# First products of two experts for half the batches computed ahead, and a new written order on all engines, in a one-core Mamba and Soft-MoE layer

## The reference, cut to what matters

```python
h = _layernorm(x) * (1 + ca) + sa
x = x + ga * mamba(h)              # in-projection, conv of 4 taps, silu, decay, out-projection
h = _layernorm(x) * (1 + cb) + sb
xn = rmsnorm(h); sn = rmsnorm(slot_embeds)
logits = einsum('bnd,esd->bnes', xn, sn)
dispatch = softmax(logits, axis=1); combine = softmax(logits over e and s)
slots = einsum('bnd,bnes->besd', xn, dispatch)
h = gelu(einsum('besd,edh->besh', slots, w1) + b1)      # the "first products", 128 -> 512
eo = einsum('besh,ehd->besd', h, w2) + b2
x = x + gb * einsum('bmd,bnm->bnd', eo, combine)
```

## Time and profile before

| | |
|---|---|
| median of 3 runs | 234.22 us (234.08 to 236.19) |
| profiled execution, its own time | 231.47 us |
| its span (first to last instruction) | 229.5 us |
| PE busy | 208.5 us, 91% of the span |
| DVE busy | 138.8 us, 60% |
| ACT busy | 120.3 us, 52% |
| POOL busy | 60.8 us, 26% |
| second pass, about | 84 to 155 us of the span |
| stage two, about | 155 to 212 us |

### The profile page before, as it was taken

How to read it: one execution, slowest core, us unless ns; L and a number is a source line. 1 busy time by engine, 2 the same in 40 slices (tenths; PEclk the granted TensorE clock), 3 DMA queues, 4 the chain that set the end, 5 groups by cost and what they waited for, 6 DMA issues and landing times.

```text
span 229.5 us, 4239 instructions
## 1 busy us (share of the span) xinstructions
PE 208.5 (91%) x1575; PEld 150.0 (65%) x1575; DVE 138.8 (60%) x364; ACT 120.3 (52%) x264; POOL 60.8 (26%) x147
## 2 busy tenths in 40 slices
PE   3898988996789899998996799989999999999995
PEld 2544565665458695565664478776774947759995
DVE  3795869799899966878889784730040220402663
ACT  2869898531557875699530666647417053270000
POOL 6443886015632401886015610000000000000000
PEclk9999997999999999999999999999999999999999
DMA  6404000300320000000600000005222142200122
GB/s 186 118 4 140 1 0 5 94 3 0 124 106 3 0 0 0 4 0 2 188 0 1 0 3 0 0 3 171 60 57 80 49 121 64 69 26 0 49 69 69
DMA packets 15344, 10.72 MB, mean 47 GB/s; under 512 B 1773, under 2 KB 13654, under 8 KB 15326
## 3 DMA queue, kind: packets, MB, share of 16 engines
q1 hardware_dynamic: 15100, 10.31, 14.9%
q10 hardware_dynamic: 226, 0.16, 0.3%
HBM read 9.34 MB, written 1.07 MB: 45 GB/s over the span
## 4 chain that ended last, share of the span: by engine, by line
PE 71%; DVE 11%; ACT 10%; DMA 3%; issue 2%; POOL 1%; ACTq 1%; DVEq 0%
PE bank L577 30%; PE bank L922 12%; PE bank L904 11%; PE bank L761 4%; PE bank L814 3%; PE bank L750 2%; DVE xcT L1310 2%; ACT zsT L1067 2%; PE bank L829 2%; DMA vec_nat<-ffn_slot_norm_gamma_dram 1%; ACT xhT L1073 1%; PE bank L835 1%; PE bank L860 1%; PE bank L883 1%; ACT L1067 1%
## 5 line engine op out<-in xcount | busy, mean ns | idle before, releaser
L1445 DVE TENSOR_TENSOR eo<-bank,seg_e 128x512 f32<-128x512 f32 x8 | 5.5, 692 | 47.9 <-PE bank L922 47.9
L922 PEld LDWEIGHTS bank<-w_sb,zsT 128*64 128x64 f32 x256 | 27.8, 137 | 3.0 <-issue 3.0
L922 PE MATMUL bank<-w_sb,zsT 128*64 128x128 f32 x256 | 28.8, 273 | 0.0
L922 PE MATMUL bank<-w_sb,xcT 128*64 128x128 f32 x256 | 28.8, 273 | 0.0
L922 PEld LDWEIGHTS bank<-w_sb,xcT 128*64 128x64 f32 x256 | 27.8, 137 | 0.0
L904 PE MATMUL bank<-slotsT,w_sb 128*128 128x512 f32 (+1 forms) x64 | 26.1, 558 | 0.2 <-ACT zsT L1141 0.2
L1141 ACT ACTIVATE zsT<-bank,vecT 128x512 f32<-128x512 f32 x16 | 10.7, 687 | 24.9 <-PE bank L904 24.9
L577 PE MATMUL bank<-xnT,winT 128*128 128x512 f32 x48 | 23.0, 607 | 0.7 <-ACT BT L1054 0.7
L490 POOL TENSOR_TENSOR root<-root,neg_half 128x2 f32<-128x2 f32 (+1 forms) x24 | 20.3, 847 | 2.0
L904 PEld LDWEIGHTS bank<-slotsT,w_sb 128*128 128x128 f32 x64 | 11.4, 190 | 12.6 <-issue 12.1
L1310 DVE SCALAR_TENSOR_TENSOR xcT<-bank,convw,xcT 128x510 f32<-128x510 f32 (+2 forms) x24 | 17.3, 736 | 3.6 <-ACT xcT L1051 3.3
(11 more groups left out here) (165 smaller groups left out, 423.7 us busy)
## 6 DMA issues: line engine op xcount, KB each, us to landing
w_sb<-in_L_ffn_w_dram SPq DMA_DIRECT2D x16, 256.0 KB, 2.9
mods_bc<-mod_dram SPq DMA_DIRECT2D x4, 320.0 KB, 3.6
xin<-in_L_attn_x_dram SPq DMA_DIRECT2D x4, 256.0 KB, 3.1
out_dram<-x1tok SPq DMA_DIRECT2D x16, 64.0 KB, 1.5
mods_bc<-mod_dram SPq DMA_DIRECT2D x4, 192.0 KB, 3.2
seg_e<-mod_dram SPq DMA_DIRECT2D x1, 512.0 KB, 3.4
eo<-in_L_attn_in_proj_w_dram SPq DMA_DIRECT2D x1, 384.0 KB, 4.2
eo<-in_L_wmod_dram SPq DMA_DIRECT2D x1, 256.0 KB, 5.1
```

The lines of the kernel that those rows point to most:

```text
L922: q = nc.tensor.matmul(o[j * S:(j + 1) * S, tile_cols(b)], act_h[j][k // 2][:, k % 2, at:at + S], w2_sb[j][:, k, :], start=k == 0 and b == ...
```

## The change: what it does

1. For experts 2 and 3 (round 1 of stage two) the first products of batches 0 to 3 are made in the second pass, on PE, by `ahead_hidden(0)` and `ahead_hidden(1)`: 4 products of 256 columns each, into banks 2 and 3, and banks 6 and 7. ACT's `copy_ahead` copies the four banks to SBUF, into x's and xnT's buffers, which are free by then. In stage two `hidden(1)` makes only the other 256 columns, and ACT's `gelus` makes two activations of 256 columns where it made one of 512.
2. The two weight tiles for this are loaded by two more DMAs into xntok's buffers, ahead of the first loads of w1 in SP's list.
3. `parts` keeps its remainder in the PSUM bank instead of SBUF.
4. The turns of all five tables are new, with some waits that the new orders need (`wait_before` in three steps; `logits(0)` of the second pass waits for `copy_ahead`).

```diff
+        AHEAD, AHEAD_B = 2, B // 2
+        w1_ahead = [t[:, :, :].rearrange("p t d -> p (t d)") for t in xntok]
+        pre = [t[:, :, :].rearrange("p t d -> p (t d)") for t in xin], [t[:, :] for t in xnT]
...
+            for j in range(2):
+                wait(sp, xnT_ps, j, PASSES - 1)
+                sp.dma_start(w1_ahead[j], w1[AHEAD + j:AHEAD + j + 1, :, :].rearrange("o d h -> d (o h)")
+                             ).then_inc(w1_ahead_in[1][j], 16)
...
                         wait(pe, seg_done, j, it)
+                        if it == PASSES - 1:
+                            wait(pe, pre_done, j, 0)
...
+            def ahead_hidden(j):
+                def visit():
+
+                    wait(pe, seg_done, j, PASSES - 1)
+
+                    for i in range(2):
+                        wait(pe, slotsT_done, i, 0)
+                    wait(pe, w1_ahead_in, j, 0)
+                    for k in range(HC):
+                        q = mm(bank[4 * j + 2 + k // 2][:, tile_cols(k % 2, AHEAD_B * S)], w1_ahead[j][:, tile_cols(k)],
+                               slotsT[:, AHEAD + j, 0:AHEAD_B, :].rearrange("p b s -> p (b s)"))
+                        if k % 2:
+                            q.then_inc(pre_ps[1][j], 1)
+                return visit
...
-                    b0 = EARLY if it == 0 and j == 0 else 0
+                    e = it * 2 + j
+                    b0 = EARLY if e == 0 else AHEAD_B if e in (AHEAD, AHEAD + 1) else 0
...
+            def copy_ahead(j):
+                def visit():
+                    for n in range(HC // 2):
+                        wait(act, pre_ps, j, 0, n + 1)
+                        if j == 0:
+                            wait(act, basis_done, n, PASSES - 1)
+                        A(pre[j][n], bank[4 * j + 2 + n][:, :], ACT.Copy).then_inc(pre_done[1][j], 1)
+                return visit
...
-                        wait(act, hid_ps, j, it, k + 1)
-
+                        o, at = act_h[j][k // 2][:, k % 2, :], 0
                         if it:
                             act.wait_ge(eo_ps, 2 * it)
-                        A(act_h[j][k // 2][:, k % 2, :], bank[k][:, :], ACT.Gelu,
-                          bias=vecT[:, bass.ds(it * 2 * HC + (RB1 + j * HC + k), 1)]).then_inc(gelu_done[1][j], 1)
+                        if e in (AHEAD, AHEAD + 1):
+                            at = AHEAD_B * S
+                            A(o[:, 0:at], pre[j][k // 2][:, tile_cols(k % 2, at)], ACT.Gelu, bias=b1_of[k])
+                        wait(act, hid_ps, j, it, k + 1)
+                        A(o[:, at:], bank[k][:, at:], ACT.Gelu, bias=b1_of[k]).then_inc(gelu_done[1][j], 1)
...
-                r = dv[j][:, PP, :].rearrange("p (t h) -> p t h", h=H)
+                r = bank[4 * j + 2][:, TP * H:2 * TP * H].rearrange("p (t h) -> p t h", h=H)
...
-            visits = [((0, 4, 52, 57), statistics1), ((1, 5, 54, 59), centre1), ((2, 8, 58, 61), modulate1),
+            visits = [((0, 1, 47, 61), statistics1), ((2, 5, 54, 63), centre1), ((3, 6, 55, 68), modulate1),
```

More of the change, by code:

```diff
@@ L484, in visit @@
                 def visit(j, it):
+                    if done is var_done:
+                        wait_before(pool, xn2_done, j, it)
                     wait(pool, done, j, it, k)
@@ new lines, in _ @@
+            visits = [((2, 6, 61, 65), t_xn), ((4, 9, 64, 68), project1), ((7, 10, 66, 72), project2),
+                      ((8, 13, 69, 74), project3), ((11, 16, 70, 76), scores), ((12, 17, 71, 77), running_sums),
+                      ((14, 19, 73, 86), part_rows), ((15, 25, 75, 87), t_xh), ((18, 27, 78, 89), segment(0)),
+                      ((20, 28, 79, 90), segment(1)), ((21, 30, 80, 91), segment(2)), ((22, 31, 81, 93), segment(3)),
+                      ((23, 32, 82, 94), y_of(0)), ((24, 33, 83, 95), segment(4)), ((26, 34, 84, 96), segment(5)),
+                      ((29, 36, 85, 97), project_out(0)), ((35, 38, 88, 99), y_of(1)),
+                      ((37, 39, 92, 101), project_out(1)), ((40, 44, 102, 106), t_xn2(0)),
+                      ((41, 45, 103, 107), logits(0)), ((42, 46, 104, 108), t_xn2(1)),
+                      ((43, 48, 105, 110), t_logits(0)), ((47, 52, 109, 114), shifts(0)),
+                      ((49, 54, 111, 116), fill_slots(0)), ((50, 55, 112, 117), logits(1)),
+                      ((51, 56, 113, 118), t_slots(0)), ((53, 58, 115, 120), t_logits(1)),
+                      ((57, 60, 119, 122), shifts(1)), ((59, 63, 121, 123), fill_slots(1)),
+                      ((62, 67, 124, 125), t_slots(1))]
@@ L905, in hidden @@
                                          slotsT[:, it * 2 + j, b0:, :].rearrange("p b s -> p (b s)"),
-                                         start=b0 == 0, stop=True, skip_group_check=True).then_inc(hid_ps[1][j], 1)
+                                         start=e > 0, stop=True, skip_group_check=True).then_inc(hid_ps[1][j], 1)
             def outputs(it):
@@ L1134, in gelus @@
+            pipeline(act, visits, once=[(1, scale_win), (2, slot_squares), (5, unit_slots), (6, small_rows),
+                                        (7, copy_wo), (10, copy_sn), (13, lambda: rsm_rows(1).then_inc(s_act0, 1)),
+                                        (97, copy_ahead(0)), (98, copy_ahead(1))])
             def gelus(it):
                 for j in range(2):
+                    e = it * 2 + j
+                    b1_of = [vecT[:, RB1 + e * HC + k:RB1 + e * HC + k + 1] for k in range(HC)]
@@ L1191, in statistics1 @@
                 wait(dve, x_in, j, it)
+                wait_before(dve, var_root_done, j, it)
                 statistics_of(j, it, 0, range(TP), own_norm1, var_done)
@@ L1438, in _ @@
-            pipeline(dve, visits, once=[(3, vectors), (7, rows_of_mods), (9, small_vectors)])
+            visits = [((0, 1, 47, 61), statistics1), ((2, 5, 54, 63), centre1), ((3, 6, 55, 68), modulate1),
+                      ((7, 10, 66, 71), unit1), ((9, 12, 70, 73), dt_in), ((11, 13, 72, 74), conv_and_softplus),
+                      ((14, 16, 75, 80), parts), ((15, 23, 76, 87), dt_times_x), ((17, 24, 77, 90), weigh(0)),
+                      ((18, 25, 78, 91), weigh(1)), ((19, 26, 79, 92), weigh(2)), ((20, 30, 81, 95), gate(0)),
+                      ((21, 31, 82, 96), weigh(3)), ((22, 33, 83, 97), weigh(4)), ((27, 34, 84, 98), weigh(5)),
+                      ((28, 35, 85, 99), x1(0)), ((29, 37, 86, 100), statistics2(0)),
+                      ((32, 40, 88, 102), modulate2(0)), ((36, 41, 89, 103), gate(1)), ((38, 43, 93, 106), x1(1)),
+                      ((39, 45, 94, 107), statistics2(1)), ((42, 48, 101, 108), modulate2(1)),
+                      ((44, 49, 104, 109), unit2(0)), ((46, 53, 105, 112), unit2(1)),
+                      ((51, 56, 110, 113), token_max(0)), ((52, 57, 111, 114), slot_max(0)),
+                      ((58, 62, 115, 118), norm_slots(0)), ((59, 64, 116, 119), token_max(1)),
+                      ((60, 65, 117, 120), slot_max(1)), ((67, 69, 121, 122), norm_slots(1))]
@@ L1440, in _ @@
+            pipeline(dve, visits, once=[(4, vectors), (8, rows_of_mods), (50, small_vectors)])
             dve.wait_ge(s_rows_bc, 48)
```

62 lines of the change are left out of this document (20 added, 42 removed).

## The result

The changed kernel takes 234.5 us (median of 20 runs, 231.5 to 236.3), beside 233.25 us for the kernel before on the same chip. The ratio is 1.008 with an interval of 1.005 to 1.011: 0.8% slower, about 1.9 us. (The ratio leaves out the runs of each kernel that lie more than 1.5% above its fastest, 7 of 20 for the kernel after; the medians of all runs differ by less, 1.25 us.) Forecast were 232.9 us and a gain of 1.3 us. The time lies inside the range, but the sign is wrong.

The account below looks back on a forecast made before the run. PE was taken as the bound (71% of the chain), with some 4.7 us idle in the second pass, where DVE is late. Tail -3.2, second pass +2.2, first pass and join -0.3: 234.22 - 1.3 = 232.9 us, range 229.9 to 235.9.

Parts of the forecast that it names:

- term A: Stage two's tail: hidden(1) makes half its columns, so outputs(1) starts 3.3 us earlier, of which 3.2 us counted as gain.
- that is 0.36 us a piece: In the tail: ScalarE's time for each 256-column activation, taken from a 0.38 us copy with overlap, was put at 0.36 us.
- T + 0.2: In the tail, T being the end of outputs(0): ScalarE's activations start here, and outputs(1) at T + 3.8.
- Term B: Second pass: 3.4 us of added PE products, partly hidden in idle time, and DVE's new order cost +2.2 us.
- last gate of pair 1: Second pass, hand replay of DVE's new order: this gate ends at 127.4, with the first decay at 105.39.
- work ahead is hidden: Rival, second pass: 4.7 us of PE idle time hides the 3.4 us of added products; 230.7 us, chance 0.36.
- DVE pays for the deeper stagger: Rival, both passes: pair 1's DVE chain starts late, its last gate ending after 128.3; +2.4, or 236.6 us; chance 0.14.
- term C: First pass and join to the second: a later start, a wait that goes and a better clock, together -0.3 us.
- by the replay the first decay comes about 0.5 late and the end of the pass 0.7: First pass: pair 1's statistics delay the first centring by 2.2 us, and ACT's and DVE's queues absorb most of it.
- The wait at 79.27: At the join: the 0.60 us wait for the maxima should go, counted as -0.6 us.
- the clock didn't fall at 36 us: First pass: shorter PE idling before the first segment may keep the clock at 2.4 GHz, counted as -0.4 us.
- `parts` in the bank: Second pass, pair 1: three steps beside POOL drop to 0.17 us, 1.4 us of DVE, half of it lost.

Follow-up runs that it names:

- e4_turns: The changed kernel with the work ahead taken out, keeping the new turns and the remainder in the bank; 237.0 us, ratio 1.022 to the kernel before.
- e9_two_back: The changed kernel with two first-pass VectorE visits put back: pair 1's x1(0) behind pair 0's gate(1), x1(1) behind unit2(0); 231.4 us, ratio 0.995.
- e1_parts: The kernel before with one line changed: the remainder of `parts` lies in the bank, not in dv; ratio 1.0035.
- e7_start: The changed kernel with pair 1's first-pass statistics put back behind pair 0's normalisation; ratio 1.011 to the kernel before.
- e10_routing: The changed kernel with the second pass's order from the first xn2T transposes on (logits, shifts, slots) as before; ratio 1.0066.
- e3_both: The kernel before with the work ahead and the remainder in the bank, every turn as before; ratio 1.001.
- e6_placed: The kernel before with its old turns, the remainder in the bank and the work ahead placed where PE waits in the trace; 230.7 us, ratio 0.989.
- e15_swaps_in_before: The kernel before with only pair 1's first-pass x1(0) moved ahead of pair 0's gate(1) and x1(1) ahead of unit2(0); 234.7 us, ratio 1.011.
- e14_unit: The changed kernel with only pair 1's first-pass x1(1) put back behind pair 0's unit2(0); ratio 0.9975 to the kernel before.

## Why the prediction was wrong, and where it was right

**The account.** Tail -2.7 (rows above). The second pass +2.4: from the second decays' table load to the last slots' copy before takes 51.25 us, e4_turns 52.25 and after 53.65, so 1.0 of it is the new turns and 1.4 the products ahead. The two swaps +3.1 (e9_two_back against after, by the ratios). These sum to +2.8, and +1.9 was measured. They come from single traces and from runs, and the sum isn't closed: 0.9 us of it is open. e1_parts and e7_start show no part of it, and e10_routing none that can be told.

With the two swaps back the kernel is 0.5% or 1.2 us faster than before, and 1.3 were forecast for the whole change. That it comes so near is in part luck, since term A was 0.5 us too large.

**Term A was right, 0.5 us too large.** Its size was off in the step "that is 0.36 us a piece": the pieces from SBUF take 0.40. And the first piece from the bank starts at T + 0.67 (176.93), since a late product of 0.64 stands before it, where I had let ScalarE start at T + 0.2. The nine pieces from there take 3.5 us and the hand-over 0.14: T + 4.3.

**Term B was right.** +2.2 foreseen, +2.1 in the trace up to the first shifts and +2.4 up to the last slots' copy; last gate of pair 1 ending 21.7 us after the first decay (130.43 and 0.69), 22.0 replayed; ahead(0) before the last y and ahead(1) before the last out-projection, each about 1.9 us. The rival *work ahead is hidden* is refuted by e3_both, and e6_placed shows what it would have needed: not the sum of idle time, but products that stand in it. *DVE pays for the deeper stagger* falls: that last gate would have had to end later than 22.9 after the decay. (Its price of +2.4 left out term C's -0.3.)

**Term C is the step that failed**: "by the replay the first decay comes about 0.5 late and the end of the pass 0.7". The first half is about right (36.53 for 35.94). The second isn't: I replayed VectorE's new order number by number only for the second pass and carried the first over. There the order had changed at two places that my replay never compared, both behind the decays. For these term C had nothing, and they are the largest single cost: 3.1 us by the runs of e9_two_back, and 1.1% when put into the kernel before by e15_swaps_in_before. From the first table load to the end of the first logits after takes 29.9 us and e9_two_back 25.6. Of these 4.3 us, 2.5 stand before the logits (26.1 for 23.6), and 1.8 are the logits at the low clock. The wait at 79.27 did go, and the clock didn't fall at 36 us, but both were small beside the swaps. In this execution the clock fell at 60 instead, where the chain runs through PE's logits.

**`parts` in the bank** gives steps of 0.17 and 0.18 us, as expected, and beside a busy GpSimd too. In e1_parts all five of pair 1's steps in the second pass (107.09 to 108.11) stand beside one GpSimd step. Two of them:

```profile
106.93 1.26 POOL L510 TENSOR_TENSOR basis<-basis,xin 128x512 f32<-128x512 f32 x1
107.30 0.18 DVE L1348 TENSOR_TENSOR bank<-bank,Q 128x16 f32<-128x16 f32 x1
107.52 0.17 DVE L1349 CAST Q<-bank 128x16 bf16<-128x16 f32 x1
```

In the earlier trace rows L1349 takes 0.66 us beside the same step, with its source in SBUF. In after a step on `dv` that stayed in SBUF shows the same:

```profile
99.23 1.25 DVE L1347 TENSOR_SCALAR dv<-dv 128x16 f32<-128x16 f32 x1
```

It took 1.25 us while GpSimd's L522 ran from 99.17 to 100.44; the shortest of the same line took 0.16. The Trainium skill (page "GPSIMD Engine Reference", section "1. Specifications") says that VectorE and GpSimd share their interfaces to SBUF, and that a VectorE step contends for them if it runs in a 2-port mode or has two inputs in SBUF. The trace agrees that a step on SBUF is held, with those 1.25 us; L1347 has one input there, and no row shows the mode it ran in.

**The clock.** Grouped by the mean granted clock of a run, at 0.993 the medians are 232.6 us before (47 runs), 233.7 after (5), 231.5 with the two visits back (5). So at the same mean clock the swaps cost some 2.2 us, near the 2.5 by which the traces of these two kernels differ up to the first logits. The kernels ran on several chips, but the kernel before has 232.5 to 232.8 on each of four at this clock. The rest of the 3.1 goes with the mix of clocks, since more runs of the changed kernel have a lower mean: 14 of 20 at or below 0.985, before 20 of 104, e9_two_back 2 of 12. Whether the swaps cause this isn't shown. All seven profiles with the second swap have a low stretch between 58 and 70 us, and of the ten without it three. But e15_swaps_in_before has the swaps and no run at or below 0.985. And e14_unit, without the second swap, has 8 of 12 runs at or below 0.985, from another stretch near 12 to 24 us. It stays open.

## What to carry to other kernels

A wait isn't a place: work moved "into idle time" must stand in the queue just where the engine waits, or it stands ahead of work that is ready. e3_both and e6_placed have the same instructions, with the same idle time to fill, and lie 1.2% apart by their ratios.

When an order is given by a table, compare every engine's list around every wait of the bound engine, in every pass. A visit that waits for the other pair, put one place ahead of one that is ready, cost 1.7 us here at the same mean clock and 2.5 by the ratios; undoing one or two such numbers is a cheap experiment, and undoing the two here turned a slower kernel into one 0.5% faster than before.

## What of the hardware was not expected

TensorE's granted clock went to 0.50, the 1.2 GHz level, where its last two pauses for another engine were 1.01 and 1.05 us, with 1.11 us of work in the 2 us window from 58 to 60:

```profile
58.00:60.00 2.00, 1.11 (x8) 0.91 (x8) 1.17 (x4) 0.69 (x4) 0.95 (x3) 1.00 0.20 56
...
62.00:64.00 2.00, 2.00 (x3) 0.67 (x2) 1.89 (x11) 0.57 (x1) 1.72 (x4) 0.50 0.02 9
```

e9_two_back was busy 1.03 us in that same window after a pause of 1.47, and kept 1.00. What PE did just before doesn't decide it alone, so from a single profile it can't be told whether an edit saved or cost a clock stretch. Runs of the kernel before have a median of 230.9 us at a mean clock of 1.000 (18 runs) and of 234.3 at 0.978 (8).
